# Attention scores from float32r products of 12-bit pieces in 64-row tiles, with the masks kept as 128-row products

## The chip, the cores and the metric

The kernel runs on one core of a Trainium2 chip, in one launch. The metric is the device time in microseconds; three runs of the kernel before took 1177.02, 1177.39 and 1177.69 us (median 1177.39).

## The reference

A chain of eight blocks on x of shape (4, 512, 128), each followed by a residual sum and a layer norm: a gated recurrence with an MLP, a ternary MLP, causal attention, a top-2 mixture of experts, attention with linear position biases, a small per-channel network, attention with one extra "void" key, a second mixture of experts. The change concerns the three attentions (16 heads of 8 dimensions, 4 sequences of 512 tokens):

```python
scores = einsum('bhqd,bhkd->bhqk', q, k) * scale      # attention 0: causal, -inf above the diagonal
scores = scores + slopes * minimum(k - q, 0)          # attention 1: position bias, no causal mask
dots = concat(q k^T, q void_k) / temperature          # attention 2: one more key, no mask
out = softmax(scores) @ v
```

The products must hold float32 accuracy, so q and k are cut into pieces with few bits and the products of pieces are summed.

## The kernel before

One program for each engine, tied by semaphores. A sequence of 512 tokens is a chunk; four heads of it are a unit, so an attention has 16 units. A unit has eight jobs, two for each tile of 128 queries or keys, and a job covers two heads. All engines walk the same slots: slot t makes the row maxima of job t + 14 (`maxima`, L839), the scores of job t (`scores`, L862), and in odd slots the products of weights and values of a finished tile of keys (`values`, L883). Slot 8n - 5 turns the maxima of unit n (`turned`, L856), slot 8u + 13 turns the sums of unit u (`output`, L896). Slots 8u + 9 on ScalarE copy the accumulator (`evacuation`, L1308). The first 14 slots, with maxima alone, lie among the last steps of the layer in front, in an order written out as strings of digits (`LAYER0_TENSOR_TURNS` and others, L145 to L158; R is a slot).

Maxima are products of bf16 pieces over 32 rows, two heads in two 32-row tiles at once (L849), plus in attention 0 a product of the identity with the mask (L852). VectorE reduces each pair of banks (L1663), GpSimd cuts the maxima in two (L2508, L2510), TensorE turns them (L859), VectorE copies them to `mT` (L1677), and GpSimd sends them as two rows of the query operand (L2535). Scores are products of keys and queries over 128 rows of bf16 (L876), 72 of products of pieces, up to 9 for the position bias and 2 for the maxima, the others blank; in attentions 0 and 1 each is followed by its mask (L879). The score products use three PSUM banks in turn, each freed by the exponential of ScalarE (L1299):

```python
def score_bank(use):
    if use >= 3:
        pe.wait_ge(exped, use - 2)
    return 4 + use % 3
```

The queue of TensorE is in order, so what stands behind such a wait waits too. Values are float32 in four 32-column tiles (L892).

Operands: ScalarE writes each of q and k twice, as bf16 and float32 (`operand`, L1228), VectorE makes two more pieces in three operations (`splits`, L1521), SyncE spills the pieces to DRAM (three transfers for maxima, four for scores) and loads them replicated (`maxima_load` L486, `score_load` L493). Before each attention ScalarE blanks the operand rows (`blank_rows`, L1223, two copies of 4096 elements) and SyncE writes the constant rows (`constant_rows`, L537). At the start constant images are built in DRAM (L603 to L613).

Of the kernel before, what the change touches and what calls it, by code (L numbers as in the profile page):

```python
# [7 lines left out]
F32 = mybir.dt.float32  # L8
BF16 = mybir.dt.bfloat16
U32 = mybir.dt.uint32  # L10
# [5 lines left out]
P = 128  # L16
# [59 lines left out]
NCOMBO = 72  # L76
NLIN = 9
# [19 lines left out]
PREP_V = "{0}.lo {0}.mid {0}.low {0}.v"  # L97
# [106 lines left out]
def build_program(nc, args, out):  # L204
    ctx = ExitStack()
    with ctx:
# [14 lines left out]
        LANE = 8192  # L221
        arena = sb("arena", [P, B * LANE])
# [22 lines left out]
        class Lane:  # L245


            def __init__(self, c):
# [18 lines left out]
                self.parts = view(arena, at + 6656, [2, 3, S], BF16)  # L267
                self.pieces = view(arena, at + 6656, [6, S], BF16)
# [10 lines left out]
        OQ = [view(arena, slot_at[s], [R, S], BF16) for s in range(NB)]  # L279
        OK = [view(arena, slot_at[s] + 1024, [R, S], BF16) for s in range(NB)]  # L280
        operands = [view(arena, lanes[c].big, [2, 2 * R * S], BF16) for c in range(2)]
        max_at = [lanes[0].big + 4096, lanes[1].big + 4096, 0, LANE]
        MQK = [view(arena, max_at[s], [2 * S], BF16) for s in range(NB)]
        MQ = [view(arena, max_at[s], [S], BF16) for s in range(NB)]
        MK = [view(arena, max_at[s] + 256, [S], BF16) for s in range(NB)]
# [22 lines left out]
        masks = ("causal_kq", "causal_qk", "alibi_kq", "alibi_qk", "tri")  # L308
# [11 lines left out]
        negm, nmp = sb("negm", [P, 2, R, CT]), sb("nmp", [P, 2, R, CT], BF16)  # L320
        mT, rden = sb("mT", [32, NB, P], BF16), sb("rden", [P, R * CT])
# [12 lines left out]
        of_head, vks, turned_wq, vkw = sb("of_head", [P, H]), sb("vks", [P, H]), sb("turned_wq", [P, D]), sb("vkw", [P, H])  # L334
# [16 lines left out]
        score_q = nc.dram_tensor("score_q", (B, 3, HD, H, S), BF16, kind="Internal").ap()  # L351
        score_k = nc.dram_tensor("score_k", (B, HD, 3, H, S), BF16, kind="Internal").ap()
        max_parts = nc.dram_tensor("max_parts", (2, B, 4, HD, H, 2, S), BF16, kind="Internal").ap()
        fixed_rows = nc.dram_tensor("fixed_rows", (2, NLIN + 2, 2, R, S), BF16, kind="Internal").ap()
        rows16 = nc.dram_tensor("rows16", (2, NLIN + 2, S), BF16, kind="Internal").ap()
        max_rows16 = nc.dram_tensor("max_rows16", (3, 8, S), BF16, kind="Internal").ap()
# [14 lines left out]
        zeroed, cast16, shared_in, bias_in = (  # L371
            sem(n) for n in ("zeroed", "cast16", "shared_in", "bias_in"))
        rows_in, blanked = [sem(f"rows_in{c}") for c in range(2)], [sem(f"blanked{c}") for c in range(2)]
        max_spilled, score_spilled = [sem(f"max_spilled{c}") for c in range(B)], [sem(f"score_spilled{c}") for c in range(B)]
        max_in = [sem(f"max_in{s}") for s in range(NB)]
        score_in = [sem(f"score_in{s}") for s in range(NB)]
        image_rows, blank_rows = sem("image_rows"), sem("blank_rows")
# [87 lines left out]
        def key_rows(a):  # L465
            return NCOMBO + (NLIN if ATT[a]["lin"] else 0)

# [14 lines left out]
        def sync_program():  # L482
# [3 lines left out]
            def maxima_load(a, u):  # L486
                s, which = u % NB, 1 if ATT[a]["lin"] else 0
                c, heads = u // G, slice(u % G * R, u % G * R + R)
                if u % G == 0:
                    sp.wait_ge(max_spilled[c], 16 * 3 * (a + 1))  # L490
                sp.dma_start(MQK[s], max_parts[which, c, :, :, heads].rearrange("j d r n q -> r (j d) (n q)")).then_inc(max_in[s], 16)

# [198 lines left out]
        def tensor_program():  # L691
# [127 lines left out]
            def attention(a):  # L819
# [19 lines left out]
                def maxima(job):  # L839
                    u, qt, rp = job // 8, job % 8 // 2, job % 2  # L840
                    s, b = u % NB, ring_banks("max", job)
                    if job < 2:
                        banks_left(job)
# [1835 lines left out]
```

## Time and profile before

| | |
|---|---|
| median of the runs | 1177.39 us |
| profiled execution, its span from first to last instruction | 1195.9 us; the profile gives no other time of it, and nothing around the span |
| TensorE busy / VectorE / ScalarE / GpSimd | 1013.1 / 779.4 / 662.2 / 363.6 us |
| TensorE's mean granted clock | 0.916 of full speed (2.4 GHz) |
| attention 0, scores run | 172.4 to 345.0 us of the span |
| attention 1, scores run | 558.8 to 754.5 us |
| attention 2, scores run | 847.5 to 1040.0 us |
| loads of one unit: score_q, score_k, max_parts | 288, 288, 256 KB |
| spills of one chunk: max_parts three of 256 KB, score_k three of 128 KB, score_q 384 KB | 1536 KB |
| GpSimd's issue of the row of maxima (L2535) | 0.64 us |

The profiled execution is 1.6% longer than the median of the runs. Busy times overlap between engines. A matmul's record is longer than its streaming, so the difference of two starts on TensorE is the better measure of its cost.

### The profile page before, as it was taken

To read this page: it belongs to the slowest core of one execution; us is meant where nothing else is said; L and a number is where in the kernel's file an instruction comes from. 1 tells how busy PE (TensorE), PEld (TensorE's weight loads), DVE (VectorE), ACT (ScalarE), POOL (GpSimd) and SP (SyncE) were. 2 spreads that over 40 slices of the span, in tenths; PEclk is the share of its full clock that TensorE was granted. 3 is DMA by queue.
4 is the path that set the end of the run, shared out by engine and by line. 5 is a ranking of instruction groups with operands and counts; after the bars stand their busy time and mean duration, and the time that the engine had idled before them with its cause. 6 is when DMAs were issued, how large, how long until landed. Compare 5 with 4: busy or idle time off the path is not lost.

```text
span 1195.9 us, 18814 instructions
## 1 busy us (share of the span) xinstructions
PE 1013.1 (85%) x6456; PEld 502.9 (42%) x6517; DVE 779.4 (65%) x1614; ACT 662.2 (55%) x1282; POOL 363.6 (30%) x587
## 2 busy tenths in 40 slices
PE   5599789999979899456999999798999998876993
PEld 2267534544436566332333333485323232233551
DVE  5966486768733300388888885429888889646565
ACT  4664536655544345152777777582477776753341
POOL 7535411101532244320000002210112223556554
PEclk9799779999988899865999999898799999999897
DMA  5910224334611120233333220003333423212232
GB/s 142 181 46 1 94 86 144 126 113 129 168 38 36 55 67 18 65 95 126 100 117 125 65 79 5 1 1 126 112 119 119 134 89 96 63 33 62 56 87 80
DMA packets 98374, 101.70 MB, mean 85 GB/s; under 512 B 13354, under 2 KB 80571, under 8 KB 98199
## 3 DMA queue, kind: packets, MB, share of 16 engines
q1 hardware_dynamic: 86169, 89.28, 25.3%
q0 software_dynamic: 6432, 8.18, 2.4%
q10 hardware_dynamic: 5680, 3.04, 0.9%
q8 instruction: 53, 0.87, 0.3%
q14 instruction: 40, 0.33, 0.1%
HBM read 66.60 MB, written 38.09 MB: 88 GB/s over the span
## 4 chain that ended last, share of the span: by engine, by line
PE 67%; DVE 14%; ACT 8%; issue 5%; DMA 3%; another core or an unknown queue 1%; POOL 1%; SPq 0%; ACTq 0%; DVEq 0%; POOLq 0%
PE PS L892 13%; PE PS L876 12%; PE PS L849 8%; PE PS L698 6%; PE PS L703 6%; DVE negm L1663 5%; PE PS L1170 4%; PE PS L1053 3%; PE PS L879 3%; PE PS L1047 2%; PE PS L852 2%; ACT arena L1299 2%; PE PS L900 2%; PE PS L1186 2%; ACT arena L1226 1%
## 5 line engine op out<-in xcount | busy, mean ns | idle before, releaser
L1299 ACT ACTIVATE arena<-PS 128x512 f32<-128x512 f32 (+3 forms) x768 | 363.0, 549 | 190.6 <-PE PS L879 121.8
L1663 DVE TENSOR_REDUCE negm<-PS 128x2 f32<-128x1024 f32 (+3 forms) x384 | 405.2, 1088 | 94.3 <-PE PS L849 46.1
L876 PE MATMUL PS<-arena 128*128 128x512 bf16 (+3 forms) x707 | 221.1, 363 | 12.1 <-ACT arena L1299 8.0
L892 PE MATMUL PS<-arena,VPAD 128*32 128x512 f32 (+3 forms) x1536 | 187.7, 559 | 0.1
L849 PE MATMUL PS<-arena 32*128 32x512 bf16 (+3 forms) x768 | 144.3, 376 | 33.1 <-DVE negm L1663 27.4
L849 PEld LDWEIGHTS PS<-arena 32*128 32x128 bf16 x768 | 36.3, 91 | 216.7 <-DVE negm L1663 112.9
L876 PEld LDWEIGHTS PS<-arena 128*128 128x128 bf16 x768 | 69.9, 98 | 123.5 <-issue 57.3
L2508 POOL CAST nmp<-negm 128x16 bf16<-128x16 f32 x48 | 9.3, 195 | 363.9 <-DVE negm L1663 244.1
L698 PE MATMUL PS<-arena,W 128*128 128x512 f32 x144 | 83.2, 711 | 11.5 <-ACT arena L1217 9.0
L703 PEld LDWEIGHTS PS<-W,arena 128*128 128x128 f32 x640 | 81.0, 206 | 13.8 <-issue 6.3
L703 PE MATMUL PS<-W,arena 128*128 128x128 f32 x640 | 82.8, 291 | 3.3 <-DVE arena L1607 3.0
L1170 PE MATMUL PS<-VPAD,arena 128*128 x92 | 53.3, 663 | 11.4 <-DVE arena L2174 5.5
L2535 POOL DMA_DIRECT2D arena<-mT x48 | 30.7, 639 | 101.1 <-DVE mT L1677 78.9
L1937 DVE TENSOR_TENSOR arena<-PS,arena 128x512 f32<-128x512 f32 x8 | 5.5, 692 | 84.2 <-PE PS L1053 84.2
L879 PE MATMUL PS<-b_alibi_kq,b_ident 128*128 128x128 bf16 x256 | 56.9, 222 | 4.0 <-issue 2.2
L2473 POOL DMA_INDIRECT rows_y<-arena,name x46 | 46.6, 1013 | 37.4 <-DVE arena L2187 17.9
L1407 ACT ACTIVATE arena<-PS,eb 128x320 f32<-128x320 f32 x64 | 33.8, 527 | 39.9 <-PE PS L1047 38.0
L2391 POOL DMA_INDIRECT rows_y<-arena,back x40 | 39.2, 981 | 54.6 <-DVE arena L1940 40.0
L879 PE MATMUL PS<-b_causal_kq,b_ident 128*128 128x128 bf16 x256 | 52.5, 224 | 2.8 <-issue 2.1
L1217 ACT COPY arena<-PS 128x512 f32<-128x512 f32 x39 | 22.7, 587 | 48.8 <-PE PS L694 45.3
L1047 PE MATMUL PS<-arena,VPAD 128*128 128x320 f32 x128 | 44.2, 472 | 3.4 <-ACT arena L1402 1.7
L698 PEld LDWEIGHTS PS<-arena,W 128*128 128x128 f32 x144 | 29.3, 225 | 41.9 <-issue 26.0
(334 smaller groups left out, 1541.3 us busy)
## 6 DMA issues: line engine op xcount, KB each, us to landing
arena<-score_q SPq DMA_DIRECT2D x48, 288.0 KB
arena<-score_k SPq DMA_DIRECT2D x48, 288.0 KB
arena<-max_parts SPq DMA_DIRECT2D x48, 256.0 KB
max_parts<-arena SPq DMA_DIRECT2D x36, 256.0 KB, 2.9
score_k<-arena SPq DMA_DIRECT2D x36, 128.0 KB
score_q<-arena SPq DMA_DIRECT2D x12, 384.0 KB
arena<-rows_y SPq DMA_DIRECT2D x16, 256.0 KB, 4.3
arena<-slots SPq DMA_DIRECT2D x46, 65.0 KB
```

What stands on the lines that cost most here:

```text
L698: pe.matmul(bank(b), w, x, start=True, stop=True).then_inc(*T.did(c, name))
L703: mm = pe.matmul(PS[:, b, j * D:(j + 1) * D], lhs(f, j), rhs(f), start=(f == 0), stop=(f == nf - 1))
L849: mm = pe.matmul(PS[:, b + i, 0:nk], MQ[s][rows, qt * P:(qt + 1) * P], MK[s][rows, 0:nk], start=True, stop=True)
L876: mm = pe.matmul(PS[:, b, q0:S], OK[s][:, r, kt * P:(kt + 1) * P], OQ[s][:, r, q0:S], start=True, stop=True)
L879: mm = pe.matmul(PS[:, b, kt * P:(kt + 1) * P], bf["ident"][:], bf[o["kq"]][:], start=False, stop=True, skip_group_check=True)
L892: mm = pe.matmul(PS[32 * r:32 * r + 32, 7, q0:S], VP[:, u, kt, r, :], PB[:, kt % 2, r, q0:S], start=(kt == 0), stop=True, skip_group_check ...
L1047: pe.matmul(PS[:, (L.A, L.B)[h], 0:HALF], W1E[:, e, n * P:(n + 1) * P], L.exT[:, h * HALF:(h + 1) * HALF], start=True, stop=True).then_inc ...
L1170: pe.matmul(bank(2 * (t % 3) + 1), xT3[t % 4], WE3[:, bass.ds(experts[t] * 768, 512)], start=True, stop=True).then_inc(multiplied3, 1)
L1299: act.activation(PB[:, kt % 2, r, q0:S], PS[:, 4 + use % 3, q0:S], ACT.Exp, scale=slope(u % G, r) if o["slope"] else 1.0).then_inc(exped, 1)
L1663: vec.tensor_reduce(negm[:, u % 2, 2 * rp:2 * rp + 2, qt], PS[:, 2 * (use % 2):2 * (use % 2) + 2, 0:nk], AX.X, ALU.max, negate=True).then_ ...
L2391: pool.indirect_dma_start(rows_y, bass.IndirectOffsetOnAxis(ap=lanes[k].back[:, r, j:j + 1], axis=0), lanes[k].ey[:, j, :], None, bounds_c ...
L2473: pool.indirect_dma_start(rows_y, bass.IndirectOffsetOnAxis(ap=name3[:, i:i + 1], axis=0), y3[i], None, bounds_check=2 * B * S - 1, oob_is ...
```

## The change

The pieces of q and k become two, of 12 significant bits each (`HIGH_BITS`), held as float32 and multiplied as float32r. A head then needs 2 x 2 x 8 = 32 rows of products, 8 for the position bias and 2 for the maxima: 42 rows. Two heads stand beside each other, at rows 0 and 64 of the operands. The same operands serve maxima (40 rows) and scores (42 rows), so the separate operands of the maxima, their spills and loads go. The score products of both heads of a job are issued first and their masks after them; masks stay 128-row bf16 products with the identity. The position bias of the diagonal tile is now carried by rows for both products, with a corrected matrix of its own for the scores. No operand rows are blanked any more; the constant rows come from one array in the inputs. The diff, cut to its core:

```diff
-NCOMBO = 72
-NLIN = 9
+PRODUCTS, NLIN = 32, 8
+HIGH_BITS = 0xFFFFF000
...
+        operands = [nc.alloc_sbuf_tensor_at(f"operands{c}", [P, 2, 2, 2, S], F32R, offset=arena_at + 4 * slot_at[2 * c]) for c in range(2)]
+        OQ = [operands[s // 2][:, s % 2, 0] for s in range(NB)]
+        OK = [operands[s // 2][:, s % 2, 1] for s in range(NB)]
...
+            def operand_load(a, u):
...
+                for h in range(2):
+                    rows, heads = slice(64 * h, 64 * h + PRODUCTS), slice(u % G * R + 2 * h, u % G * R + 2 * h + 2)
+                    sp.dma_start(OQ[s][rows]..., score_q[c, :, :, heads]...).then_inc(score_in[s], 16)
+                    sp.dma_start(OK[s][rows]..., score_k[c, :, :, heads]...).then_inc(score_in[s], 16)
...
             def spills_and_first_loads(a, tag):
-                max_spills(0, tag, a)
+                for n in range(2):
+                    spills(0, tag, n)
                 constant_rows(a, 0)
-                maxima_load(a, 0)
-                score_spills(0, tag, a)
-                maxima_load(a, 1)
-                score_load(a, 0)
-                score_load(a, 1)
+                operand_load(a, 0)
+                operand_load(a, 1)
                 constant_rows(a, 1)
-                maxima_load(a, 2)
-                score_load(a, 2)
+                operand_load(a, 2)
...
                 def maxima(job):
...
-                    for i in range(2):
-                        rows = slice(32 * (2 * rp + i), 32 * (2 * rp + i) + 32)
-                        mm = pe.matmul(PS[:, b + i, 0:nk], MQ[s][rows, qt * P:(qt + 1) * P], MK[s][rows, 0:nk], start=True, stop=True)
+                    for h in range(2):
+                        rows = slice(64 * h, 64 * h + PRODUCTS + NLIN)
+                        mm = pe.matmul(PS[:, b + h, 0:nk], OQ[s][rows, rp, q], OK[s][rows, rp, 0:nk], start=True, stop=True)
...
                 def scores(job):
...
-                    for i in range(2):
-                        r, b = 2 * rp + i, score_bank(score_use[a, job] + i)
-                        mm = pe.matmul(PS[:, b, q0:S], OK[s][:, r, kt * P:(kt + 1) * P], OQ[s][:, r, q0:S],
-                                       start=True, stop=True)
-                        if o["kq"]:
-                            mm = pe.matmul(PS[:, b, kt * P:(kt + 1) * P], bf["ident"][:], bf[o["kq"]][:],
-                                           start=False, stop=True, skip_group_check=True)
-                        mm.then_inc(scored, 1)
+                    b, mm = [], []
+                    for h in range(2):
+                        rows = slice(64 * h, 64 * h + PRODUCTS + NLIN + 2)
+                        b.append(score_bank(score_use[a, job] + h))
+                        mm.append(pe.matmul(PS[:, b[h], q0:S], OK[s][rows, rp, kt * P:(kt + 1) * P], OQ[s][rows, rp, q0:S], start=True, stop=True))
+                    if o["kq"]:
+                        for h in range(2):
+                            mm[h] = pe.matmul(PS[:, b[h], kt * P:(kt + 1) * P], bf["ident"][:], bf[o["kq"]][:],
+                                              start=False, stop=True, skip_group_check=True)
+                    for h in range(2):
+                        mm[h].then_inc(scored, 1)
...
             def operand(c, tag, n, scale, bias):
-                act.activation(L.parts[:, n, 0, :], bank(b), ACT.Identity, scale=scale, bias=bias)
                 act.activation(L.pair[:, n, :], bank(b), ACT.Identity, scale=scale, bias=bias).then_inc(*A.did(c, f"{tag}.{part}"))
...
             def splits(c, tag):
-                vec.tensor_tensor(L.pair, L.pair, L.parts[:, :, 0, :], ALU.subtract).then_inc(*V.did(c, tag + ".lo"))
-                vec.wait_ge(*V.at(c, tag + ".lo"))
-                vec.tensor_copy(L.parts[:, :, 1, :], L.pair).then_inc(*V.did(c, tag + ".mid"))
-                vec.wait_ge(*V.at(c, tag + ".mid"))
-                vec.tensor_tensor(L.parts[:, :, 2, :], L.pair, L.parts[:, :, 1, :], ALU.subtract).then_inc(*V.did(c, tag + ".low"))
+                vec.tensor_scalar(L.pieces[:, :, 0].bitcast(U32), L.pair.bitcast(U32), HIGH_BITS, None, ALU.bitwise_and).then_inc(*V.did(c, tag + ".high"))
+                vec.wait_ge(*V.at(c, tag + ".high"))
+                vec.tensor_tensor(L.pieces[:, :, 1], L.pair, L.pieces[:, :, 0], ALU.subtract).then_inc(*V.did(c, tag + ".low"))
...
-                    pool.dma_start(OQ[s][KR:KR + 2]..., mT[:, s, :]).then_inc(max_row[s], 16)
+                    for h in range(2):
+                        at = 64 * h + PRODUCTS + NLIN
+                        pool.dma_start(OQ[s][at:at + 2]..., mT[16 * h:16 * h + 16, u % 2, :]).then_inc(max_row[s], 16)
```

`spills` sends one of q and k in two transfers of 256 KB after the last split; a chunk spills 1024 KB. A unit loads 512 KB in four transfers. `mT` has two slots instead of four. The maxima of a unit wait for the loaded operands and, for the first unit of each half, for the constant rows; `blank_rows` and its six calls go.

## Rows read from the trace of the kernel before

**Rows 1.** Busy time by stretch: TensorE, its loads, VectorE, ScalarE, GpSimd, clock, DMA.
```profile
172.40:345.00 172.60, 162.89 (x1555) 79.81 (x1571) 119.18 (x242) 99.72 (x262) 35.56 (x68) 0.96 0.42 128
558.80:754.50 195.70, 190.26 (x1293) 61.84 (x1315) 144.27 (x160) 142.29 (x272) 19.90 (x49) 0.97 0.25 82
847.50:1040.00 192.50, 177.85 (x1040) 52.24 (x1058) 162.71 (x255) 137.76 (x279) 57.04 (x130) 0.98 0.35 109
```

**Rows 2.** Timeline (start, duration), attention 2: a pair of slots, TensorE and ScalarE.
```profile
880.38 1.06 PE L892 MATMUL PS<-arena,VPAD 128*32 128x512 f32 x8
881.38 0.39 PE L849 MATMUL PS<-arena 32*128 32x512 bf16 x2
881.70 0.39 PE L876 MATMUL PS<-arena 128*128 128x512 bf16 x1
...
882.18 0.60 ACT L1299 ACTIVATE arena<-PS 128x512 f32<-128x512 f32 x1 [1.23 <-PE PS L876]
...
882.84 0.39 PE L876 MATMUL PS<-arena 128*128 128x512 bf16 x1
883.16 0.64 PE L892 MATMUL PS<-arena,VPAD 128*32 128x512 f32 x4
```

**Rows 3.** Timeline, attention 1: one slot on TensorE and ScalarE's start.
```profile
640.64 0.39 PE L849 MATMUL PS<-arena 32*128 32x512 bf16 x2
...
641.19 0.22 PE L879 MATMUL PS<-b_alibi_kq,b_ident 128*128 128x128 bf16 x1
...
641.46 0.22 PE L879 MATMUL PS<-b_alibi_kq,b_ident 128*128 128x128 bf16 x1
641.62 0.39 PE L849 MATMUL PS<-arena 32*128 32x512 bf16 x2
...
641.51 2.06 ACT L1299 ACTIVATE arena<-PS 128x512 f32<-128x512 f32 x4 [0.89 <-PE PS L879]
```

**Rows 4.** Attention 0: timeline of a slot, the accumulator copy, exponentials grouped by form.
```profile
194.14 0.39 PE L849 MATMUL PS<-arena 32*128 32x512 bf16 x2
194.46 0.29 PE L852 MATMUL PS<-b_causal_qk,b_ident 128*128 128x128 bf16 x2
194.58 0.38 PE L876 MATMUL PS<-arena 128*128 128x512 bf16 x1
...
195.22 0.43 PE L892 MATMUL PS<-arena,VPAD 128*32 128x128 f32 x8
...
196.03 0.59 ACT L1312 COPY arena<-PS 128x512 f32<-128x512 f32 x1
...
L1299 ACT ACTIVATE arena<-PS 128x384 f32<-128x384 f32 x64 | 26.9, 512 | 6.4 <-PE PS L879 6.4
```

**Rows 5.** Timeline of float32 transposes and what follows; float32 weight loads by form.
```profile
907.68 0.66 PE L983 MATMUL PS<-c_ident,arena 128*128 128x128 f32 x4
908.27 0.39 PE L849 MATMUL PS<-arena 32*128 32x512 bf16 x2
...
642.49 0.61 PE L900 MATMUL PS<-c_ident,arena 128*128 128x128 f32 x4
643.03 1.06 PE L892 MATMUL PS<-arena,VPAD 128*32 128x512 f32 x8
...
L703 PEld LDWEIGHTS PS<-W,arena 128*128 128x128 f32 x640 | 81.0, 206 | 13.8 <-issue 6.3 <-DVE arena L1607 4.9 <-ACT arena L1221 1.2
```

**Rows 6.** In front of the attentions: blanking copy, TensorE's waits, a split's operation.
```profile
135.19 3.59 ACT L1226 COPY arena<-zeros 128x4096 f32<-128x4096 f32 x1
...
122.76 3.75 PE L698 MATMUL PS<-arena,wqkv 128*128 128x512 f32 x4 [2.48 <-ACT arena L1217]
139.31 3.78 PE L698 MATMUL PS<-arena,wqkv 128*128 128x512 f32 x4 [4.39 <-ACT arena L1217]
805.56 1.98 PE L698 MATMUL PS<-arena,W 128*128 128x512 f32 x4 [2.67 <-ACT arena L1217]
...
L1528 DVE TENSOR_TENSOR arena<-arena 128x1024 bf16<-128x1024 f32 x12 | 14.7, 1225 | 0.4
```

More of the change, by code:

```diff
@@ L8 @@
 F32 = mybir.dt.float32
+F32R = mybir.dt.float32r
 BF16 = mybir.dt.bfloat16
@@ L96 @@
 NORM_G = "{0}.va {0}.rs"
-PREP_V = "{0}.lo {0}.mid {0}.low {0}.v"
+PREP_V = "{0}.high {0}.low {0}.v"
 EXPERTS_A = " ".join(f"x{r}.xT x{r}.xT4 " + " ".join(f"x{r}.h{i}" for i in range(8)) for r in range(2))
@@ L221, in build_program @@
         LANE = 8192
+        arena_at = (nc.sbuf_base + 31) // 32 * 32
         arena = sb("arena", [P, B * LANE])
@@ L484, in load @@
                 sp.dma_start(dst, src).then_inc(s, 16)
[L486 to L491, printed above, removed]
-            def score_load(a, u):
-                s, c, heads = u % NB, u // G, slice(u % G * R, u % G * R + R)
+            def operand_load(a, u):
+                s, c = u % NB, u // G
                 if u % G == 0:
@@ L549, in score_spills, with spills @@
-            def score_spills(c, tag, a):
+                sp.wait_ge(*(T.at(c, "t.sum"), V.at(c, "cb.tot"), T.at(c, "ch.out"))[a])
+                for h in range(2):
+                    rows = slice(64 * h + PRODUCTS, 64 * h + PRODUCTS + NLIN + 2)
+                    load(rows_in[c], operands[c][rows].rearrange("x s n p q -> x s (n p q)").bitcast(F32),
+                         fixed_rows[1 if ATT[a]["lin"] else 0].unsqueeze(1).broadcast_to([NLIN + 2, 2, 4 * S]))
+            def spills(c, tag, n):
@@ L1221, in activated @@
                 act.activation(dst, bank(b), func, **kw).then_inc(*A.did(c, name))
-            def blank_rows(a, c):
-                act.wait_ge(*PO.at(WHOLE, "zeros"))
-                act.wait_ge(*(T.at(c, "t.sum"), V.at(c, "cb.tot"), T.at(c, "ch.out"))[a])
-                act.copy(view(arena, lanes[c].big, [2 * R * S]), zeros[:, 0:1].broadcast_to([P, 2 * R * S])).then_inc(blanked[c], 1)
             def operand(c, tag, n, scale, bias):
@@ L1417, in combine_and_prep @@
                 void_weights()
-                for c in range(2):
-                    blank_rows(1, c)
                 act.wait_ge(*V.at(WHOLE, "bq"))
@@ L2646, in layout @@
     pos = np.arange(S)
[L2647 to L2655 removed]
+    rows = np.zeros((2, NLIN + 2, 2, S), f)
     for s in range(4):
         own, behind = pos // P == s, pos // P > s
[L2658 to L2662 removed]
+        rows[1, s, 0][behind], rows[1, s, 0][own] = 1, 0.5
+        rows[1, s, 1][own], rows[1, 4 + s, 1][own] = pos[own] % P, 1
+        rows[1, 4 + s, 0][behind] = -(pos[behind] % P) - P * (pos[behind] // P - s)
+        rows[1, 4 + s, 0][own] = -0.5 * (pos[own] % P) - 32
+    rows[:, NLIN:, 1] = 1
+    o["c_fixed"] = np.ascontiguousarray(np.repeat(rows[:, :, :, None], 2, 3).reshape(2, NLIN + 2, 4 * S))
     return o
```

155 lines of the change are left out of this document (49 added, 106 removed).

## The prediction

> **What bounds the kernel now.** I read the granted clock first, then the busy table by stage, then each attention instruction by instruction on TensorE and ScalarE, and last the gaps in front of each attention. In all three attentions TensorE is busy 92 to 97% of the time at a mean granted clock of 0.96 to 0.98, VectorE 69 to 85%, ScalarE 58 to 73% [rows 1]. These stretches, where scores run, are 561 us of 1195.9. A busy TensorE need not be the bound, so I looked at what lets each instruction start. The work goes in pairs of slots A and B: maxima, scores, maxima, scores, then one block of values.
>
> In attention 2 (no masks) the pair is a loop through ScalarE [rows 2]: values start 880.38, maxima A 881.38 (1.00 later), scores A 881.70 (0.32), exponential of A's first head 882.18 (0.48), second score product of B 882.84 (0.66: it needs the bank which that exponential frees), values again 883.16 (0.32). Together 2.78 us. A product of 512 columns streams in 0.22: the 0.32 after maxima holds 0.10 more. This 0.10 comes wherever the height or width of the tile changes; I call it a switch. In attention 1 [rows 3] the slot takes 0.98 (640.64 to 641.62): maxima and switch 0.32, twice score and mask 0.27, last the mask's 0.06 and a switch 0.10. The pair is 2 x 0.98 + 1.00 = 2.96. ScalarE's loop would be 1.00 + 0.32 + 0.22 + 0.32 (mask start to exponential, 641.19 to 641.51) + 0.66 = 2.52 at B's second score, and TensorE arrives there at 1.00 + 0.98 + 0.32 + 0.27 = 2.57, just behind. So attention 1 is bound by TensorE with ScalarE 0.05 away, attention 2 by the loop. In attention 0 [rows 4] a slot is maxima, switch, two masks (0.12), then score and mask twice, switch.
>
> **What the change does in steady state.** I take a float32r product at one column per cycle, as bf16: 0.22 for 512 columns, both heads of a pair beside each other in rows 0 to 63 and 64 to 127, as the two 32-row maxima products run today (x2 in 0.22, rows 2). No row shows float32r. The bound below is zero extra; the bound above is float32 (rival 2). A slot then spends one score time, not two. But two things stand against it. The mask products stay 128 rows, so there is a switch on each side of them; and both masks come after both scores, so the first exponential waits for both.
>
> Attention 2: no masks, so maxima and scores share a tile height and one switch goes on the loop: 2.78 - 0.10 = 2.68. The saved score product of B is shadow: B's second score waits for the exponential anyway. 64 pairs x 0.10 = 6.4; I take -4 since VectorE, already 85% busy there, and the copy of the accumulator hold some pairs.
>
> Attention 1: 1.00 + 0.22 (maxima) + 0.22 + 0.10 (scores, switch) + 0.32 (mask to exponential) + 0.66 (exponential, bank free) + 0.22 + 0.10 + 0.12 + 0.10 (B's second score, switch, masks, switch) = 3.06 against 2.96. TensorE alone would need 2 x (0.22 + 0.22 + 0.10 + 0.12 + 0.10) + 1.00 = 2.52, but the exponential starts no earlier than today and frees B's bank no earlier: the gain is spent waiting. 64 x 0.10 = +6.4.
>
> Attention 0: with m and s for the streaming of maxima and scores, a slot is m + 2s + 0.43 now (0.21 + 0.43 + 0.43 = 1.07; rows 4 show 194.14 to 195.22, 1.08). After it is m + s + 0.64: four switches, not two. For key tiles 0 to 3, s = 0.21, 0.16, 0.11, 0.05 and m = 0.21, 0.05, 0.11, 0.16: now 1.07, 0.80, 0.76, 0.69, after 1.06, 0.85, 0.86, 0.85. Twice the sum: 6.64 to 7.24, +0.60 per unit of eight slots. Then the wait of B's second score: the exponential and hand-over (0.66 for 512 columns; 0.51 + 0.06 for 384, rows 4; by the same step 0.42 + 0.06 for 256) less 0.21 less m: 0.24, 0.31, 0.16, none. Now the same wait is 0.05 in one pair. The accumulator copy (0.59, rows 4) delays either kernel's second pair. +0.60 + 0.66 = +1.26 per unit, x16 = +20.
>
> Weight loads: after a switch four float32 transposes take 907.68 to 908.27 = 0.59, after a mask in the same tile height 642.49 to 643.03 = 0.54 [rows 5]: a float32 weight load shows about 0.05 when it cannot be hidden. On the path this falls once per pair in attentions 1 and 2 (A's maxima) and about ten times per unit in attention 0: 64 x 0.05 x 2 + 160 x 0.05 = +14. Bounds: 0, and 0.21 each (the length of a float32 weight load, rows 5).
>
> The Trainium skill, TensorE: Matmul & The Clock Gate, section Weight-path perf modes, says that the fast weight load is given only to types other than FP32, and section LDWEIGHTS puts a load at columns / 1.2, 107 ns. By that (an estimate from the page) each load would show 0.11 where I take 0.05, and the sum would be 16 us longer. The trace has 0.05 for whole transposes; whether a float32r load counts as FP32 no run here shows.
>
> Steady sum: 20 + 6.4 - 4 + 14 = +36.
>
> **What the change does between the attentions.** The blanking copies on ScalarE go (3.6 us each, six [rows 6]), one of two evacuations of each operand, and one of three VectorE operations of a split (1.23 of 3.2 [rows 6]; the bit operation that replaces another I take like the 0.69 cast before it, up to 1.23). Before attention 0 TensorE waits 2.48 and 4.39 us for transposed inputs behind blanking copies; freed of them it waits about nothing and about 1 [rows 6]: -2.5 and -3.5; two splits in the ramp -2.4: -8. Before attention 1 the two copies end as the first transposed input arrives (the transpose waited for VectorE), so nothing goes; splits and evacuation -3. Before attention 2 TensorE waits 2.67 for the second input [rows 6], which goes, and one split in the ramp: -4, with the evacuation -5. The first load: spills of 1 MB instead of 768 KB ahead of the first maxima, then 512 KB of operands instead of 256, but without the 768 KB beside them; Ahead of the first maxima SyncE now issues four spills, two row and four operand transfers where it issued three, one and one; the single load no longer shares the queue with four more spills. I take 0, bounds -2 and +3 per attention (five issues of 0.6). For later units the load starts ten slots ahead, over 12 us. The start-up transfers that go had nobody waiting. GpSimd issues two row transfers per unit, not one (0.6 each); a unit's scores come five slots later, over 5 us: hidden. If that cover fails, each unit waits about 1 us. Sum -16, bounds -8 and -22.
>
> **The sum.** 1195.9 + 36 - 16 = 1216 in the profiled execution, a ratio of 1.017. The runs' median, 1177.39, lies 1.6% under that execution; the same ratio gives 1197.
>
> **Rivals.**
> 1. Changing between 64 and 128 rows costs nothing; only 32-row and 32-column tiles do. All switches in the rows are of those kinds, which speaks for it; that it comes both ways and with both types speaks against. Attention 1: 3.06 less the switches after each pair of scores, 2.86, -6; attention 0: slots m + s + 0.22, but the pair is then the exponential's loop, about -0.2 per unit, -3; attention 2 -4; with -16: -29, 1149. Faster.
> The Trainium skill, TensorEngine Tiling (Array Packing), section Key Properties, says that changing the tiling mode, not just the tile, drains TensorE, without a number; by that rule this rival falls and the forecast's 0.10 stands for 64 rows too. The trace agrees for 32 rows.
> 2. Float32r streams at two cycles a column, as each instruction of every float32 row: eight values instructions, four at a time, take 0.99 [rows 2], 0.43 per 512 columns. Every maxima and score pair on the loop is 0.22 longer: three per pair of slots in attentions 1 and 2 (128 pairs x 0.65 = 83), and in attention 0 three of mean length 0.13 per pair plus what stays of the wait (64 x 0.45 = 29). +112 on the forecast without its 5 of overlap: 1300.
> 3. Weight loads show 0.15 in place of 0.05: 28 more, and after each wait too, as much again: 1225 to 1255.
> 4. Faster through the gaps: with no exposed loads (-14), the transitions at their good bound (-6) and VectorE no hindrance in attention 2 (-2), 1175; a tie.
>
> **Chances.** Forecast 0.52 (its own range 1184 to 1222), rival 1 0.17, rival 2 0.11, rival 3 0.13, rival 4 0.07. The 80% range leaves out most of rival 2 and the lower half of rival 1: 1152 to 1258. What a measurement can tell here is 0.2%, 2.4 us. Faster: rival 1, half of rival 4 and a little of the forecast's low side, 0.22; same 0.04; slower 0.74.
>
> **What would show it.** In the changed profile: maxima to scores in attention 2 0.22 apart and the pair at 2.68 (right), 0.43 apart (rival 2). In attention 1 B's second score waiting for the exponential by about half a microsecond, the pair at 3.0 to 3.1. In attention 0 maxima to mask 0.32, mask to score 0.22, score to mask 0.32, a unit 1.2 to 1.7 longer; score to mask 0.22 is rival 1. First maxima of attention 0 six us earlier. I am wrong if both heads' products do not run beside each other, if B's second score is not held by ScalarE, or if attention 0 is not longer.

## The result, and the profile after

The changed kernel takes 1369.6 us (median of 4 runs, 1364.6 to 1378.8) against 1177.2 (4 runs): a ratio of 1.166, 95% interval 1.161 to 1.171. The forecast said slower, 1197, with a range of 1152 to 1258; the sign was right, the size was far off. The profiled execution has a span of 1368.3 us (1195.9 before), TensorE's mean granted clock is 0.809 (0.916), and TensorE is busy 1195.7 us (1013.1).

By the starts of maxima and scores the 172 us between the two spans split so:

| stretch, us | before | after |
|---|---|---|
| start to the first maxima of attention 0 | 149.5 | 149.5 |
| its 14 slots of maxima alone | 23.5 | 21.7 |
| attention 0, first to last score | 180.3 | 283.2 |
| to the first maxima of attention 1 | 180.8 | 189.3 |
| its maxima alone, then its scores | 24.8, 194.1 | 23.9, 226.6 |
| to the first maxima of attention 2 | 67.0 | 73.9 |
| its maxima alone, then its scores | 27.6, 208.3 | 28.9, 241.6 |
| the rest | 140.0 | 129.7 |

So 103 of the 172 lie in attention 0. The rest of 140.0 does not belong to the kernel before as such: of all kernels in this document, the three timed beside a kernel before of 1196.0 us (the last three runs below) have 138 to 141 there too, and all others 127 to 130. That is 12 of the 20 us by which the difference of the runs, 192, exceeds that of the spans, 172; where the other 8 lie is not known. The stretches of [rows 1] end 8 and 16 us before the last scores of attentions 0 and 2 (at 353.3 and 1055.9); over the whole stretches the clock before was 0.96 and 0.98 as well. Busy time by stretch of the changed kernel, the three attentions and three pieces of attention 0 (columns as in [rows 1]: length, PE, PEld, DVE, ACT, POOL, clock, DMA share, GB/s):

```profile
171.20:454.40 283.20, 283.20 (x1664) 129.53 (x1663) 127.45 (x266) 107.68 (x275) 47.75 (x87) 0.63 0.22 59
667.70:894.30 226.60, 222.45 (x1307) 82.63 (x1307) 147.19 (x160) 147.51 (x270) 27.72 (x64) 0.92 0.17 46
997.00:1238.60 241.60, 220.10 (x1146) 87.82 (x1144) 171.83 (x291) 151.82 (x308) 71.62 (x154) 0.82 0.24 66
...
210.00:245.00 35.00, 35.00 (x292) 17.43 (x291) 20.47 (x32) 18.47 (x49) 4.66 (x12) 1.00 0.28 78
280.00:315.00 35.00, 35.00 (x178) 14.34 (x176) 12.96 (x20) 12.31 (x30) 3.10 (x8) 0.50 0.14 39
385.00:420.00 35.00, 35.00 (x174) 15.88 (x172) 13.92 (x32) 10.80 (x29) 15.74 (x21) 0.51 0.50 127
```

Read PE and clock together. In attention 0 TensorE's records leave no gap in the whole stretch and the granted clock is 0.63, where [rows 1] had 0.96. The clock has two levels, 2.4 and 1.2 GHz, so the time at the lower one is 2 x (1 - 0.63) x 283 = 210 us of 283. In 35 us at 1.00 the engine gets through 292 matmuls, in 35 us at 0.50 through 178, of the same program. No gap is recorded, so the busy column shows nothing of this. The Trainium skill, TensorE: Matmul & The Clock Gate, Part 1, ties the full clock to a TensorE that is kept busy; here it is busy all the time by its records and mostly at half clock, so by this trace busy is not enough, and the measurement decides.

Attention 1 is the counterexample to keep in mind. Its products have the same 40 and 42 rows, all of 512 columns, with masks of 128 rows between, and from 703.5 on it ran at full clock:

```profile
703.50:894.00 190.50, 187.31 (x1170) 69.57 (x1170) 128.06 (x141) 130.14 (x239) 24.63 (x56) 1.00 0.16 43
```

The same slot (key tile 0, compare [rows 4]) on TensorE at full and at half clock (start, duration; differences of starts are the cost):

```profile
219.77 0.50 PE L815 MATMUL PS<-operands 40*128 40x512 f32 x2
220.20 0.28 PE L818 MATMUL PS<-b_causal_qk,b_ident 128*128 128x128 bf16 x2
220.41 0.50 PE L840 MATMUL PS<-operands 42*128 42x512 f32 x2
220.85 0.28 PE L843 MATMUL PS<-b_causal_kq,b_ident 128*128 128x128 bf16 x2
221.06 0.50 PE L815 MATMUL PS<-operands 40*128 40x512 f32 x2
...
299.24 0.79 PE L815 MATMUL PS<-operands 40*128 40x512 f32 x2
299.96 0.40 PE L818 MATMUL PS<-b_causal_qk,b_ident 128*128 128x128 bf16 x2
300.29 0.80 PE L840 MATMUL PS<-operands 42*128 42x512 f32 x2
301.02 0.40 PE L843 MATMUL PS<-b_causal_kq,b_ident 128*128 128x128 bf16 x2
301.34 0.79 PE L815 MATMUL PS<-operands 40*128 40x512 f32 x2
```

At full clock the slot is 221.06 - 219.77 = 1.29 (1.08 before, forecast 1.06): product to mask 0.43 where the forecast had 0.32, mask to product 0.21 as forecast. At half clock it is 2.10. The shortest units of attention 0 (from the first values of a unit's first key tile to those of the next unit, all at full clock) take 12.44 us, 210.03 to 222.47, against 10.08 before, 185.14 to 195.22. Attention 2 at full clock, a pair of slots on TensorE (compare [rows 2]):

```profile
1093.72 1.06 PE L857 MATMUL PS<-arena,VPAD 128*32 128x512 f32 x8
1094.71 0.50 PE L815 MATMUL PS<-operands 40*128 40x512 f32 x2
1095.05 0.40 PE L840 MATMUL PS<-operands 42*128 42x512 f32 x2
1095.29 0.40 PE L815 MATMUL PS<-operands 40*128 40x512 f32 x2
1095.53 0.40 PE L840 MATMUL PS<-operands 42*128 42x512 f32 x1
1096.19 0.50 PE L840 MATMUL PS<-operands 42*128 42x512 f32 x1 [0.27 <-ACT arena L1256]
1096.62 0.64 PE L857 MATMUL PS<-arena,VPAD 128*32 128x512 f32 x4
```

Within a run of 64-row tiles a pair of float32r products takes 0.24 (1095.05 to 1095.29), both heads beside each other. The first pair behind a change of height takes 0.34 (1094.71 to 1095.05), and the product behind the wait 0.43 (1096.19 to 1096.62), of which 0.22 is streaming and 0.10 the switch to values. Each time 0.10 to 0.11 is left over, which the weight load explains (the run with bf16 reads, below). The pair is 2.90, 2.78 before. In attention 1 it is 787.40 - 784.11 = 3.29 (2.96 before, [rows 3]), with 0.85 from B's scores, held by the exponential, to their masks:

```profile
784.11 1.06 PE L857 MATMUL PS<-arena,VPAD 128*32 128x512 f32 x8
785.11 0.50 PE L815 MATMUL PS<-operands 40*128 40x512 f32 x2
...
786.33 0.92 PE L840 MATMUL PS<-operands 42*128 42x512 f32 x2
787.18 0.28 PE L843 MATMUL PS<-b_alibi_kq,b_ident 128*128 128x128 bf16 x2
787.40 0.64 PE L857 MATMUL PS<-arena,VPAD 128*32 128x512 f32 x4
```

The last wait that matters is in front of each attention, TensorE's wait for the operands of the first maxima:

```profile
149.52 0.48 PE L815 MATMUL PS<-operands 40*128 40x128 f32 x2 [7.91 <-DMA operands<-score_k]
...
643.74 0.79 PE L815 MATMUL PS<-operands 40*128 40x512 f32 x2 [12.80 <-DMA operands<-score_k]
...
968.17 0.80 PE L815 MATMUL PS<-operands 40*128 40x512 f32 x2 [11.05 <-DMA operands<-score_k]
```

In the kernel before, TensorE waited 1.00 and 1.44 us for this transfer in front of attentions 1 and 2. In front of attention 1 SyncE issued the first load 4.6 us after the first spill before, and 7.8 after (622.85 to 630.67). From the last issue of the first unit's load to the first maxima it was 6.5 us before (527.69 to 534.17), and is 11.1 after (632.66 to 643.74):

```profile
527.69 0.60 SPq L491 DMA_DIRECT2D arena<-max_parts  x1
...
632.66 0.60 SPq L486 DMA_DIRECT2D operands<-score_k  x1
```

### The profile page after: what moved, and what is told of

Its sections match the earlier page's. It is cut to its first block, busy times and chain, and to the rows that moved or that the text cites. A ratio compares the mean times of both kernels' runs of the same rounds, so it can differ in the third digit from the quotient of the medians.

```text
span 1368.3 us, 18889 instructions
## 1 busy us (share of the span) xinstructions
PE 1195.7 (87%) x6517; PEld 607.5 (44%) x6517; DVE 776.0 (57%) x1602; ACT 638.9 (47%) x1252; POOL 388.8 (28%) x631
## 4 chain that ended last, share of the span: by engine, by line
PE 73%; DVE 10%; ACT 6%; DMA 5%; issue 3%; POOL 1%; SPq 1%; POOLq 0%; DVEq 0%; ACTq 0%
PE PS L857 15%; PE PS L840 13%; PE PS L815 11%; PE PS L662 5%; PE PS L843 5%; PE PS L667 4%; PE PS L1135 3%; DVE negm L1614 3%; PE PS L1018 3%; PE PS L818 3%; DMA operands<-score_k 2%; PE PS L865 2%; ACT arena L1256 2%; PE PS L1012 2%; PE PS L1151 2%
## 5 line engine op out<-in xcount | busy, mean ns | idle before, releaser
L1256 ACT ACTIVATE arena<-PS 128x512 f32<-128x512 f32 (+3 forms) x768 | 371.2, 543 | 342.8 <-PE PS L843 251.4
L840 PE MATMUL PS<-operands 42*128 42x512 f32 (+3 forms) x768 | 255.1, 503 | 17.5 <-ACT arena L1256 14.9
L815 PE MATMUL PS<-operands 40*128 40x512 f32 (+3 forms) x768 | 208.2, 540 | 51.5 <-DMA operands<-score_k 31.8
L857 PE MATMUL PS<-arena,VPAD 128*32 128x512 f32 (+3 forms) x1536 | 231.1, 679 | 0.1
L815 PEld LDWEIGHTS PS<-operands 40*128 40x128 f32 x768 | 85.4, 220 | 235.3 <-DVE negm L1614 85.3
L840 PEld LDWEIGHTS PS<-operands 42*128 42x128 f32 x768 | 116.1, 224 | 118.5 <-ACT arena L1256 87.9
L2488 POOL DMA_DIRECT2D operands<-mT x96 | 56.8, 594 | 136.6 <-DVE mT L1628 135.1
L857 PEld LDWEIGHTS PS<-arena,VPAD 128*32 128x32 f32 x1536 | 34.9, 120 | 31.9 <-ACT arena L1256 18.5
L1471 DVE TENSOR_SCALAR X<-arena,mv,rs 128x128 f32<-128x128 f32 x128 | 41.4, 391 | 10.5 <-POOL rs L2183 10.5
```

Source lines behind the costliest of these rows:

```text
L815: mm = pe.matmul(PS[:, b + h, 0:nk], OQ[s][rows, rp, q], OK[s][rows, rp, 0:nk], start=True, stop=True)
L840: mm.append(pe.matmul(PS[:, b[h], q0:S], OK[s][rows, rp, kt * P:(kt + 1) * P], OQ[s][rows, rp, q0:S], start=True, stop=True))
L857: mm = pe.matmul(PS[32 * r:32 * r + 32, 7, q0:S], VP[:, u, kt, r, :], PB[:, kt % 2, r, q0:S], start=(kt == 0), stop=True, skip_group_check ...
L1256: act.activation(PB[:, kt % 2, r, q0:S], PS[:, 4 + use % 3, q0:S], ACT.Exp, scale=slope(u % G, r) if o["slope"] else 1.0).then_inc(exped, 1)
L2488: pool.dma_start(OQ[s][at:at + 2].rearrange("a p (t q) -> a (p t) q", t=CT), mT[16 * h:16 * h + 16, u % 2, :]).then_inc(max_row[s], 16)
```

## The experiments

The theory after these rows: most of the loss is time at half clock. Three theories stood against each other. What lowers the clock is the changes of tile height (A), or it is the 64-row float32r products by their kind (B), or the clock is no cause, and weight loads and switches are (C).

**No masks in attention 0.** `if o["kq"]` became `if o["kq"] and a`, and `if o["qk"]` `if False`. Attention 0 is then not causal.

> The changed kernel with the mask products of attention 0 left out (its scores and maxima are then not causal), so that no 128-row product stands between the 64-row ones there. Theory A (the loss is time at half the granted clock, and what lowers the clock is the change of tile height four times a slot, during which TensorE's records say busy while its array stands): attention 0 goes back to a clock of 0.95 or more, its scores run in about 165 us, and the kernel takes about 1250 us. Theory B (the loss is time at half the clock, and what lowers it is the 64-row float32r products themselves): the clock of attention 0 stays at 0.5 to 0.7, its scores take 230 us or more, the kernel about 1320. Rival C (the clock is no cause, the loss is weight loads and switches at any clock): the time falls by what the masks cost at full clock, some 5 us in each of 16 units at most, to 1290, with the clock where it was.

1317.7 us. Attention 0's scores took 234.8; no switch stood between maxima and scores any more, and the clock was no better (0.54 over the attention, 0.63 with the masks):

```profile
180.00:380.00 200.00, 196.42 (x1016) 100.38 (x1015) 109.93 (x221) 93.31 (x236) 37.99 (x73) 0.54 0.28 75
```

Theory A fell as the only cause.

**Masks in 64-row tiles.**

```diff
-for h in range(2):
-    mm[h] = pe.matmul(PS[:, b[h], kt * P:(kt + 1) * P], bf["ident"][:], bf[o["kq"]][:], ...)
+for x in range(2):
+    for h in range(2):    # halves: rows 64h to 64h+63 hold half x of the matrix
+        mm[h] = pe.matmul(PS[:, b[h], kt * P:(kt + 1) * P], halves("ident2", h, x), halves(o["kq"], h, x), ...)
```

> The changed kernel with every mask made in 64-row tiles too: two products of 64 rows for each head (the halves of identity and mask stand beside each other in both groups of rows), so that no tile height changes inside a slot, and two heads' masks run beside each other. Twice as many mask products. Theory A (the switches lower the clock): attention 0 runs at 0.9 or more, a slot of key tile 0 takes 0.8 to 0.95 in place of 1.29, attention 1's pair falls from 3.29 to about 3.0; kernel 1230 to 1260. Theory B (64-row float32r products lower it): attention 0 stays at half clock, with a unit of about 16 us in place of 19; kernel 1310 to 1340. Rival C (weight loads are what costs): eight mask products a slot each show a load, 0.05 to 0.1, and the time stays within 20 us of 1370.

1302.4 us, ratio 1.110 (1.103 to 1.117). A slot of key tile 0 took 0.85 at full clock, and attention 0 was 104 us at half clock (clock 0.77). More products, a shorter time and a better clock than without any masks: C's 20 us was wrong, and A had just fallen as the only cause, so it looked as if something in the mask products themselves helped the clock. They use all their rows. Whether the missing switches helped too this run alone can't tell; with all rows read (below) they made no difference to the clock, 0.88 with them and 0.89 without.

**Reads as bf16.** `matmul(..., OK[...], OQ[...])` became `matmul(..., high(OK[...]), high(OQ[...]))`, with `high` the upper halves.

> The changed kernel with maxima and scores reading only the upper 16 bits of each operand element, as bf16 with a stride of 4 bytes; the tiles, the order and the masks are as they were (the products are then those of 8-bit pieces). Theory A (switches): the clock of attention 0 stays at 0.5 to 0.65, kernel 1340 to 1370. Theory B (float32r in 64 rows): the clock goes back to 0.95, kernel 1230 to 1260. Rival C (weight loads of float32r cost 0.11 each where bf16 ones hide): the clock as in the changed kernel, slots 0.2 to 0.3 shorter at full clock, kernel about 1330.

1267.1 us, ratio 1.077 (1.072 to 1.083). Attention 0 was 223.2 us with 101 at half clock, attention 2 228.3 with 70. None of the three had said that: bf16 in the same tiles still lost the clock, less often (0.77 for 0.63 in attention 0, 0.97 for 0.92 in attention 1). The kind of number, or what comes with it, has a part in the clock, and is not the whole cause.

**The order of scores and masks, in the kernel before.** Both score products first, then both masks.

> The kernel before with one thing of the change: the score products of both heads of a job are issued first and both masks after them. All are 128-row bf16 products, so no switch is added. By the forecast's loop the first exponential starts one product later (0.22), and attention 1's pair goes from 2.96 to about 3.18: +14 us there; in attention 0 up to 0.2 in each of the four pairs of a unit with long rows, +5 to +10; sum 1195 to 1200 us. The rival, that TensorE hides it all, says 1177. The granted clock should be as in the kernel before, 0.96 and more in attentions 0 and 1.

1196.2 us, ratio 1.016 (1.013 to 1.020), as the forecast's loop says. A unit of attention 0 takes 10.59 us at full clock (10.08 before), 8 us in 16 units. The pair of attention 1 (2.96 in [rows 3]) is 653.51 - 650.35 = 3.16, and B's two scores take 0.66 to their masks, where two products stream in 0.44, since the second waits for its bank:

```profile
650.35 1.06 PE L896 MATMUL PS<-arena,VPAD 128*32 128x512 f32 x8
...
652.64 0.83 PE L878 MATMUL PS<-arena 128*128 128x512 bf16 x2
653.30 0.28 PE L882 MATMUL PS<-b_alibi_kq,b_ident 128*128 128x128 bf16 x2
653.51 1.07 PE L896 MATMUL PS<-arena,VPAD 128*32 128x512 f32 x8
```

**The kernel before without blanking.** This was meant for the transitions:

```diff
-mm = pe.matmul(PS[:, b, q0:S], OK[s][:, r, kt * P:(kt + 1) * P], OQ[s][:, r, q0:S], ...)
+mm = pe.matmul(PS[:, b, q0:S], OK[s][0:used, r, kt * P:(kt + 1) * P], OQ[s][0:used, r, q0:S], ...)
```

> The kernel before, with the blanking copies of ScalarE left out: score products read only the 74 rows (83 in attention 1) that hold something. This is the part of the forecast's step between the attentions that rests on the blanking alone: -2.5 and -3.5 us in front of attention 0 and -2.7 in front of attention 2, so about 1169 us. The rival, that the next wait (VectorE's splits, the last chunk's chain) takes the whole place, says 1175 to 1177. Products of 74 or 83 rows must stream as those of 128, in 0.22.

The first maxima came at 141.9 in place of 149.5, and the stretch in front of attention 2 fell from 67.0 to 63.0: the blanking was worth what the forecast said and a little more. And yet the kernel was slower, 1221.6, ratio 1.035 (1.031 to 1.039). All of it is in attention 2, whose score products read 74 rows and no longer 128 (its stretch, and a slot in its slow part):

```profile
838.80:1091.40 252.60, 244.80 (x1147) 60.43 (x1145) 173.55 (x291) 153.70 (x308) 61.23 (x137) 0.75 0.28 85
```
```profile
901.66 0.60 PE L849 MATMUL PS<-arena 32*128 32x512 bf16 x2
902.20 1.03 PE L876 MATMUL PS<-arena 74*128 74x512 bf16 x2
903.16 0.61 PE L849 MATMUL PS<-arena 32*128 32x512 bf16 x2
```

A clock of 0.75 where [rows 1] had 0.98, with the same bf16 columns in the same order. The 54 rows of zeros had held the clock up (two runs below put them back). Attentions 0 (74 rows, 128-row masks between, 0.93) and 1 (83 rows, 0.97) kept 0.9 and more. This gave theory R: fewer rows at work in the products lower the clock.

**The first loads.** Constant rows of the first half ahead of the spills, those of the second half last.

> The changed kernel with the constant rows of the first half sent ahead of the spills, and those of the second half behind the first three loads. In the changed kernel TensorE waits 7.9, 12.8 and 11.1 us for the first operands. If the constant rows standing in the queue ahead of the loads make this wait (they occupy few rows each and 160 KB), it falls by 8 to 15 us over the three attentions: 1355 to 1362. If the operand transfers themselves are slow (128 KB into 32 rows, four for a unit), less than 4 us goes: 1366 to 1370.

1358.2 us (1344 to 1383), ratio 1.151 (1.144 to 1.159) against 1.166: about 11 us, as the first branch of the expectation had it, though the two intervals nearly touch. The waits in front of the first maxima fell from 7.9, 12.8 and 11.1 to 4.5, 10.3 and 8.1, 9 us in all, so the constant rows were under a third of the wait, and most of it stands behind the spills and the operand transfers.

**Twice the scores, and a filler**, both on top of the kernel without masks in attention 0 (so neither is causal there): each score product issued again, or one 128-row bf16 product of 512 columns ahead of each pair of maxima.

> The changed kernel with the masks of attention 0 left out (as in the run without them, 1317.7 us, attention 0's scores 234.8 us of which 210 at half clock) and with each score product of attention 0 issued twice into the same bank. More work on TensorE, the same result. Theory S (the clock falls where little is streamed through the array over time, whatever the tile): the clock recovers for a good part of attention 0, which then takes 160 to 200 us; kernel 1255 to 1290, faster with more work. Theory B (64-row float32r products lower the clock by themselves): half clock throughout, 256 products more of mean 0.15 us at full clock, beside each other in pairs: +38 us at half clock, 1355.

> The changed kernel with the masks of attention 0 left out, and one 128-row bf16 product of 512 columns added ahead of each pair of maxima in attention 0 (it is overwritten). It brings back two switches and 0.22 of streaming in each of the 128 slots. Theory S (streaming over time sets the clock): clock 0.9 or more, attention 0's scores in 185 to 200 us, kernel 1270 to 1285 against 1317.7 without the filler. Theory B allows the same, since the filler is of 128 rows and bf16; together with the doubled scores it tells whether any streaming will do. If neither is true the filler is only work at half clock: +80 us, 1395.

1367.4 and 1295.9 us, beside 1317.7 with neither. The same 200 us of attention 0, first with the doubled scores, then with the filler:

```profile
180.00:380.00 200.00, 197.69 (x1037) 110.03 (x1035) 93.28 (x185) 77.03 (x196) 23.72 (x52) 0.50 0.19 53
```
```profile
180.00:380.00 200.00, 193.44 (x1254) 87.17 (x1253) 118.97 (x258) 100.81 (x266) 46.20 (x83) 0.82 0.29 78
```

More products of 42 rows: half clock throughout, and theory S fell. One bf16 product of all 128 rows: 0.82, and 22 us less time for more work. These two runs differ in rows and in kind at once; the next one changes the rows alone.

**All 64 rows read.** The products keep columns, number, kind and order; rows 40 to 61 hold zeros, which ScalarE blanks as in the kernel before.

```diff
-rows = slice(64 * h, 64 * h + PRODUCTS + NLIN)         # maxima, 40 rows
+rows = slice(64 * h, 64 * h + 62)
-rows = slice(64 * h, 64 * h + PRODUCTS + NLIN + 2)     # scores, 42 rows
+rows = slice(64 * h, 64 * h + 64)
```

> The changed kernel with its float32r products read over all 64 rows of each tile (maxima 62, scores 64; rows 40 to 61 hold zeros, blanked by ScalarE as in the kernel before, and the maxima's rows stand at 62 and 63). Same columns, same number of products, same switches, same masks; only the rows at work grow from 40 and 42 to 62 and 64. Theory R (the granted clock follows how many rows of the array are at work, after 74 rows in place of 128 took attention 2 of the kernel before from 208 to 253 us): half-clock time in attention 0 falls from 205 to under 120 us, in attention 2 from 85 to under 40; kernel 1270 to 1320. Theory B (float32r lowers it by its kind): the clock stays, the blanking costs 4 to 8 us, kernel 1370 to 1378. The duration of a product must stay (0.24 for 512 columns).

1280.9 us, ratio 1.087 (1.083 to 1.091) against 1.166, 89 us less, though the blanking is back. The three attentions:

```profile
173.10:396.70 223.60, 223.01 (x1663) 108.81 (x1663) 126.22 (x266) 107.55 (x275) 47.76 (x87) 0.88 0.27 75
609.30:826.50 217.20, 213.32 (x1307) 79.85 (x1306) 146.74 (x160) 147.39 (x270) 27.72 (x64) 0.97 0.17 48
930.10:1151.20 221.10, 194.97 (x1146) 80.43 (x1144) 171.80 (x291) 151.36 (x308) 69.99 (x152) 0.95 0.26 71
```
```profile
244.61 0.50 PE L817 MATMUL PS<-operands 62*128 62x512 f32 x2
245.04 0.28 PE L820 MATMUL PS<-b_causal_qk,b_ident 128*128 128x128 bf16 x2
245.26 0.50 PE L842 MATMUL PS<-operands 64*128 64x512 f32 x2
```

The clock is back at 0.88, 0.97 and 0.95, and product to mask is 0.43 as it was with 40 rows: only the clock changed. The unit at full clock is 12.44 us again. Theory R holds as far as it goes: rows alone brought the clock back. B fell as the only cause, and so did C, which gave the clock no part.

**All rows, and masks in 64-row tiles; blanking in the last attention alone.**

> Both: all 64 rows read, and masks in 64-row tiles (no switch inside a slot). Under theory R this is the changed kernel with its clock and without its switches: attention 0 at a clock of 0.9 or more and a unit near 10 us, scores of attention 0 in 175 to 190 us; kernel 1210 to 1250. Under theory B it stays at the 1302 of the masks in 64-row tiles, plus the blanks.

1255.9 us, ratio 1.064 (1.059 to 1.069): 6 us beyond the expectation; attention 0 had a clock of 0.89 (expected 0.9 or more) and took 205 us, not 175 to 190.

> The kernel before, blanked only in front of attention 2, where all 128 rows are read; attentions 0 and 1 read 74 and 83 rows and have no blanking. Theory R with what was measured (74 rows cost attention 2 44 us, and attention 0, with its 128-row masks, 2; the first maxima came 7.6 us earlier without the blanks): 1180 - 7.6 - 1 + 2 = about 1173 us. The rival, that the whole of the loss without blanks was a disturbed clock, says the clock of attention 2 may fall again at 128 rows: 1210 or more.

1179.9 against 1179.4, ratio 1.000 (0.998 to 1.003), not 1173. The profiled execution was the longest of the twelve (1188.3). Attention 2 had its clock and its length again (210.0), and the first maxima were at 142.6, but attention 0 took 188.0, its 74 rows between 128-row masks with more time at half clock than before (38 against 13 us). The expectation had put that at 2 us.

**Zeros by transfer; what is left of the change.** For the first, the 54 rows of attentions 0 and 2 are filled from DRAM by SyncE in the kernel before, and attention 1 reads 83 rows with no blanking:

```diff
+load(zero_in[c], operands[c][NCOMBO + 2:P], fixed_rows[0, 2:3]....broadcast_to([P - NCOMBO - 2, 2, 2 * R * S]))
```

> The kernel before with the blank rows (74 to 127) of attentions 0 and 2 filled with zeros by SyncE's transfers from DRAM in place of ScalarE's copies; all 128 rows are read there. Attention 1 reads 83 rows and has no blanking. If the rows at work set the clock, zeros that come by DMA hold it as well as those of ScalarE: attention 2's scores in 208 to 212 us, attention 0's in 180 to 183, first maxima 6 to 7.6 us earlier, before attention 2 another 3 to 4: about 1169 us. The rival: the two transfers of 0.9 MB each stand in front of the spills and take the gain back, 1177 to 1180.

> The changed kernel with all 64 rows read (1280.9 us) and, besides, maxima and scores read as bf16 (the upper 16 bits, stride 4 bytes). The same tiles, rows, order, switches and blanks; what goes is what float32r costs beside bf16. By the slots seen at full clock (key tile 0: 1.29 with float32r, 1.10 with bf16 reads, both with the same switches) the weight loads that show are worth 0.1 each after a switch: about -24 in attention 0, -14 in attention 1, -3 in attention 2, together 1240. If the switches and the wait of B's second score are what is left, the time stays at 1265 or more.

> The changed kernel with all 64 rows read, masks in 64-row tiles, and the constant rows of the first half sent ahead of the spills. From 1255.9 us without the last: the order of the first loads gave 11 us in the changed kernel (1369.6 to 1358.2), so about 1245. If ScalarE's blanking, back in this kernel, holds the constant rows anyway, the gain is under 4: 1252 to 1256.

The kernel before took 1196.0 us beside these three, so only ratios are compared. Zeros by transfer: 0.989 (0.986 to 0.993), faster than both kernels, as expected (1169 of some 1180); first maxima at 143.7, 62.9 us in front of attention 2, and both attentions at their old lengths with the zeros in place:

```profile
167.20:346.30 179.10, 170.06 (x1650) 83.80 (x1665) 122.62 (x266) 105.48 (x277) 37.54 (x70) 0.96 0.41 124
835.50:1043.30 207.80, 191.44 (x1124) 56.00 (x1143) 169.48 (x291) 151.43 (x308) 61.46 (x137) 0.98 0.34 104
```

All rows with bf16 reads: 1.045 (1.041 to 1.049) against 1.087, so float32r costs 0.042, 50 us of 1177, beside bf16 in the same tiles at nearly the same clock (attention 0 at 0.90 for 0.88, so a little of it is clock). A unit of attention 0 at full clock takes 11.38 us (213.57 to 224.95) for 12.44, the pair of attention 1 3.08 (705.48 to 708.56) for 3.29, and the pair of attention 2 988.85 - 986.15 = 2.70 for 2.90:

```profile
986.15 1.06 PE L863 MATMUL PS<-arena,VPAD 128*32 128x512 f32 x8
987.15 0.40 PE L821 MATMUL PS<-operands 62*128 62x512 bf16 x2
987.39 0.39 PE L846 MATMUL PS<-operands 64*128 64x512 bf16 x2
...
988.85 1.06 PE L863 MATMUL PS<-arena,VPAD 128*32 128x512 f32 x8
```

The best form of the change (all rows, masks in 64-row tiles, constant rows first): 1.056 (1.051 to 1.061) against 1.064 without the last. The order of the loads gave 0.008 or nothing; the change does not reach the kernel before in any form tried.

## Why the prediction was wrong

1. **The step that failed is one that is missing.** The steady sum multiplied durations from [rows 2 to 4], all at full clock, and neither the sum nor a rival asked whether the new products would keep it. They did not: the three attentions ran some 330 us at half clock, against 31 before. Reading 62 and 64 rows in place of 40 and 42 was worth 1.166 - 1.087 = 0.079, some 90 us, with the blanking paid; in the attentions it took away some 240 us at half clock and 90 us of length, 0.37 us for each. By that price the 300 us more at half clock are about 110 of the 192 us (an estimate from these runs). The rows held both halves of the warning: the attentions ran at 0.96 to 0.98 [rows 1], on score products of 128 rows [rows 2] of which attention 2 fills 74. The zeros looked like waste. Why attention 1 kept the full clock with 40 and 42 rows, once it had it, stays open.
2. **Weight loads.** The term was 0.05 each, +14, and it was mis-sized: they show 0.11 and stand at more places. Product to mask is 0.43 where streaming and switch give 0.32: 0.11 shows after each switch, in attention 0 for both products of a slot, and at B's second score after its wait too. By the run with bf16 reads the whole of float32r costs 0.042, 50 us. This is rival 3's mechanism. In a unit of attention 0 the loads are 12.44 - 11.38 = 1.06 us where the forecast had ten times 0.05. The load records are 182 ns at the least for float32r and 92 for the bf16 reads. With the loads so priced and nothing else changed the forecast would have been 1197 + 50 - 14 = 1233. The Trainium skill, TensorE: Matmul & The Clock Gate, Weight-path perf modes, gives the fast load only to types other than FP32; the forecast had left open whether float32r is one, and these records say that it is loaded slowly.
3. **The switch** between 64 and 128 rows costs 0.10 as forecast (mask to product 0.21); rival 1 is out. Float32r streams 512 columns in 0.24 with both heads side by side; rival 2 is out.
4. **The loop through ScalarE** was right. With all rows and bf16 reads, where no load shows, attention 2's pair is 2.70 (forecast 2.68), attention 1's is 3.08 (3.06), and a unit of attention 0 is 11.38 - 10.08 = 1.30 longer than before (1.26), all at full clock. Scores first and masks last alone cost 1.016, and the loop had said that for the kernel before. In attention 1 the changed kernel's 3.29 is this pair and two loads that show.
5. **The transitions.** The blanking's part was right (-7.6 and -4.0 for -6 and -2.7). The first loads were taken at 0 with bounds -2 and +3 each; the waits of 7.9, 12.8 and 11.1 us took the gain in front of attention 0 away, and the other two stretches became 8.5 and 6.9 us longer. So the -16 came out as about +14 (the six stretches outside the scores, without the rest), some of it time at half clock. The step that failed counted issues on the queue and not the time of the transfers: in front of attention 1 the first load is issued 7.8 us behind the first spill in place of 4.6, and from its last issue to the first maxima it takes 11.1 in place of 6.5.

Two small slips of the sums change nothing: rival 2's terms give 1304, not 1300, and the transitions' upper bound is -16 + 9 = -7, not -8.

From 1.087 with all rows, 0.042 is float32r beside bf16, 0.016 the order and 0.023 the 128-row masks' switches (from the run with 64-row masks): 1.006 is left, if they add up, which was not tried in one kernel. That the order costs the same in the changed kernel as in the one before was not tried either.

## What to carry to other kernels

Before a change makes TensorE's products lower (fewer rows, smaller tiles), count the granted clock of the stretch as a price: at half clock a slot took 2.10 us where it took 1.29 at full. Rows of zeros that nobody needs can be what keeps it at 1.00. Test it with the cheapest edit there is, the same products over more or fewer rows. A busy share of 100% and more wall time for the same instruction count is the sign to look for.

## What was not expected of the hardware

- The granted clock fell with TensorE busy: 0.63 over 283 us of 283 busy, with 40- and 42-row products in 64-row tiles; 0.75 with bf16 products of 74 rows (0.98 with 128, of which 54 are zeros). The level is not steady: in one attention the same products ran 35 us at 1.00 and later 35 us at 0.50.
- Added work can shorten a kernel: one 128-row bf16 product more in each of 128 slots took 1317.7 to 1295.9 us; 256 products of 42 rows more took it to 1367.4.
- Behind a change of tile height a float32r product shows 0.11 us of its weight load. Within one tile height no load shows: 512 columns take 0.24 with float32r and with bf16 reads alike.
- How many rows are enough was not settled, and rows are not all: 83 rows kept 0.97 in attention 1, 74 rows with 128-row masks between them had 0.93 and 0.90 in two runs, and attention 1 of the changed kernel ran 190 us at 1.00 on 40 and 42 rows. Its products are all of 512 columns and it has masks; attention 0 has masks and shorter products (0.63), attention 2 has the same products and no masks (0.82). No run tells these two apart.
